# GpSimd takes norms, diagonal blocks and part of a convolution in a fused two-layer kernel on Trainium2

## The reference

```
mixed   = silu(conv4(x @ W_qkv.T))          # causal, depthwise, 4 taps, 2048 channels
q, k, v = split(mixed)                      # 8 key heads (each for 2 value heads), 16 value heads, 64 wide
z, beta = x @ W_z.T, sigmoid(x @ W_b.T)
g       = -exp(A_log) * softplus(x @ W_a.T + dt_bias)
per token:  S = S * exp(g);  delta = (v - S'k) * beta;  S = S + k delta';  o = S'(q / 8)
h       = o * silu(z);  h = h * rsqrt(mean(h*h) + 1e-6) * norm_weight
out     = h @ W_out.T
```

## Time and profile before

| | us |
|---|---|
| median of three executions | 1510.51 (1510.26 to 2404.46) |
| profiled execution | 1512.68 |
| its span in the trace | 1510.9 |
| PE busy | 1284.2 (85%) |
| DVE busy | 910.1 (60%) |
| ACT busy | 726.2 (48%) |
| POOL busy | 194.1 (13%) |

### The profile page before, as it was taken

How to read it: one execution, slowest core, us unless ns; L and a number is a source line. 1 busy time by engine, 2 the same in 40 slices (tenths; PEclk the granted TensorE clock), 3 DMA queues, 4 the chain that set the end, 5 groups by cost and what they waited for, 6 DMA issues and landing times.

```text
span 1510.9 us, 26872 instructions
## 1 busy us (share of the span) xinstructions
PE 1284.2 (85%) x11048; PEld 928.8 (61%) x11048; DVE 910.1 (60%) x2365; ACT 726.2 (48%) x1353; POOL 194.1 (13%) x186
## 2 busy tenths in 40 slices
PE   2668889798898979889996959998899989989899
PEld 2355767576575756757765536665567656666566
DVE  4897888979788897969255333552445523463321
ACT  1648375665746556582541324434352354523442
POOL 5111221212112121212010010000100000000000
PEclk9768779788877978887898788998999999999999
DMA  4000000000000000010120000000000000000000
GB/s 125 4 2 5 0 2 11 2 12 1 12 1 2 11 2 8 2 32 8 54 105 8 2 1 0 1 8 1 8 0 8 1 2 8 0 1 1 1 8 7
DMA packets 15066, 17.69 MB, mean 12 GB/s; under 512 B 2567, under 2 KB 13216, under 8 KB 14560
## 3 DMA queue, kind: packets, MB, share of 16 engines
q1 hardware_dynamic: 12768, 14.09, 2.8%
q0 software_dynamic: 576, 1.76, 0.4%
q10 hardware_dynamic: 1600, 0.12, 0.1%
HBM read 13.87 MB, written 2.10 MB: 11 GB/s over the span
## 4 chain that ended last, share of the span: by engine, by line
PE 60%; DVE 25%; ACT 9%; issue 3%; POOL 1%; DMA 1%; SPq 0%; DVEq 0%; ACTq 0%
PE ps L1539 8%; PE ps L1529 8%; PE ps L1329 7%; PE ps L1094 4%; DVE arena L1880 4%; DVE arena L1883 3%; DVE arena L1797 3%; PE ps L1237 3%; PE ps L1112 3%; DVE arena L2154 2%; ACT arena L975 2%; PE ps L1631 2%; PE ps L1170 2%; PE ps L1595 2%; PE ps L1259 1%
## 5 line engine op out<-in xcount | busy, mean ns | idle before, releaser
L1797 DVE SCALAR_TENSOR_TENSOR arena<-ps,conv_w,arena 128x255 f32<-128x255 f32 (+2 forms) x384 | 163.8, 475 | 19.1 <-ACT arena L636 14.5
L937 ACT ACTIVATE arena<-ps 128x512 f32<-128x512 f32 x144 | 85.3, 597 | 180.7 <-PE ps L1529 180.7
L1539 PEld LDWEIGHTS ps<-arena 128*128 128x128 f32 x1152 | 132.6, 192 | 24.8 <-issue 9.9
L1539 PE MATMUL ps<-arena 128*128 128x128 f32 x1152 | 136.9, 277 | 7.1 <-ACT arena L937 4.1
L1529 PE MATMUL ps<-arena 128*128 128x512 f32 x288 | 134.3, 612 | 0.0
L2125 DVE SCALAR_TENSOR_TENSOR arena<-ps,gates,arena 128x128 f32<-128x128 f32 x128 | 36.0, 344 | 113.7 <-PE ps L1539 113.4
L523 POOL TENSOR_TENSOR rstd<-var_eps,half_power 128x2 f32<-128x2 f32 (+1 forms) x28 | 23.3, 833 | 621.1 <-DVE var_eps L1768 621.1
L2191 DVE TENSOR_REDUCE arena<-ps 128x8 f32<-128x2048 f32 (+1 forms) x24 | 54.8, 2292 | 62.8 <-PE ps L1595 62.8
L1529 PEld LDWEIGHTS ps<-arena 128*128 128x128 f32 x288 | 51.4, 194 | 61.0 <-issue 44.8
L1883 DVE TENSOR_TENSOR arena<-arena 128x30 f32<-128x30 f32 (+14 forms) x240 | 83.4, 348 | 8.2
L502 POOL TENSOR_TENSOR arena<-con,log_decay 128x512 f32<-128x512 f32 x64 | 67.0, 1059 | 162.6 <-PE ps L1094 62.1
(11 more groups left out here) (246 smaller groups left out, 2817.2 us busy)
## 6 DMA issues: line engine op xcount, KB each, us to landing
arena<-in_routed_up SPq DMA_DIRECT2D x1, 2048.0 KB, 10.5
arena<-in_routed_down SPq DMA_DIRECT2D x1, 2048.0 KB, 14.9
x_ln<-in_x SPq DMA_DIRECT2D x8, 128.0 KB, 2.3
arena<-in_w_mix SPq DMA_DIRECT2D x1, 1024.0 KB, 10.9
x_in<-in_x SPq DMA_DIRECT2D x8, 128.0 KB, 2.3
out_x<-x_res SPq DMA_DIRECT2D x8, 128.0 KB, 1.9
arena<-out_x SPq DMA_DIRECT2D x4, 256.0 KB, 2.7
out_x<-arena SPq DMA_DIRECT2D x4, 256.0 KB, 2.2
```

What stands on the lines that cost most here:

```text
L937: act.activation(hid1[half][:, i, :], ps[:, banks[i], :], ACT.Gelu).then_inc(s["mgelu"], 1)
L1539: mm = pe.matmul(ps[:, bank, c * P:(c + 1) * P], hid1[half][:, i, c * P:(c + 1) * P], m_down[:, e, i, :], start=(i == 0), stop=(i == HT1 - 1))
L1797: ins = dve.scalar_tensor_tensor(conv_tile(f, m)[:, sh:SEQ], ps[:, PAIR_BANK[p], j * SEQ:(j + 1) * SEQ - sh], conv_w[:, m, TAPS - 1 - sh:T ...
```

## The change

Four things are moved, and the waits around them follow.

1. `log_decays(f, 0..2)` on VectorE stand between `products(n, 3)` and `products(n, 6)` and no longer behind all products; `exponents` goes ahead of `products(n, 3)`. On TensorE `turn_norm` and `beta_decay` come first in a round, `decay_sums(n, 3)` goes from the end of a round to the start of the next, and so do the second chunk's `turn_heads`. ScalarE's list follows, and its `diagonal_blocks(n, 1)` is split: three quarters once seven products are there, the last quarter after the eighth.
2. `normalise` goes from VectorE to GpSimd, behind each `root_of_squares`.
3. `unit_blocks` goes from ScalarE to GpSimd, two blocks ahead of the first masks of sequence f and two behind the second.
4. For the channel pairs 0 to 4 (`TAPPED = 5`) ScalarE writes a second copy, the tile times its second tap (`second_tap`), into one of two buffers in `xs64`, and GpSimd adds it, one position shifted, to the seed (`add_tap`); VectorE adds two taps in place of three to these pairs.

```diff
-HT_BANKS = ((6, 6), (7, 2))
+HT_BANKS = (6, 7)
...
+TAPPED = 5
...
+        tap = [xs64[:, 8 * r:8 * (r + 1), :].rearrange("p (j b) d -> p j (b d)", j=2) for r in range(2)]
...
         @block.gpsimd
+            def add_tap(f, p):
+
+                pool.wait_ge(s["seeded"], f * MIX + 2 * p + 2)
+                pool.wait_ge(s["tapped"], 2 * (TAPPED * f + p + 1))
+                both = mix_qk[f % 2][:, 2 * p:2 * p + 2, 1:SEQ] if p < QK_TILES else mix_v[:, 0:2, 1:SEQ]
+                pool.tensor_tensor(both, both, tap[p % 2][:, :, 1:SEQ], ALU.add).then_inc(s["tap_added"], 1)
...
+            def normalise(i, c):
+
+                pool.wait_ge(s["o_rstd_ready"], CH * i + c + 1)
+                pool.tensor_tensor(hz_slot(i, c), hz_slot(i, c), over_last(o_rstd[:, :], DH), ALU.mult)\
+                    .then_inc(s["hn_ready"], 1)
+
+            def unit_blocks(n, q):
+
+                pool.wait_ge(s["uc_ready"], n + 1)
+                after(pool, "e_psum", 4 * n)
+                r = slice(BLOCK * q, BLOCK * (q + 1))
+                pool.tensor_scalar(um[r, :, r], uc[r, :, :], -1.0, None, ALU.mult).then_inc(s["um_blocks"], 1)
...
                 if has_i:
                     root_of_squares(i, 0)
+                    normalise(i, 0)
+                if has_f:
+                    for p in range(TAPPED):
+                        add_tap(f, p)
+                if has_i:
                     root_of_squares(i, 1)
+                    normalise(i, 1)
+
+                if has_n:
+                    pool.wait_ge(s["gm_ready"], CH * NB * (n + 1))
+                    after(pool, "hn_ready", CH * (i + 1))
+                    if has_f:
+                        pool.wait_ge(s["tap_added"], TAPPED * (f + 1))
+                    unit_blocks(n, 2)
+                    pool.wait_ge(s["um_blocks"], QUADS * n + 1)
+                    unit_blocks(n, 3)
+                    pool.wait_ge(s["um_blocks"], QUADS * n + 2)
...
-                if has_f:
-                    for k in range(NB + 1):
+                if has_f:
+                    masked_decays(f, 0)
+                    masked_decays(f, 1)
+                    pool.wait_ge(s["gm_ready"], CH * NB * f + 2)
+                if has_n:
+                    unit_blocks(n, 0)
+                    pool.wait_ge(s["um_blocks"], QUADS * n + 3)
+                    unit_blocks(n, 1)
+                    pool.wait_ge(s["um_blocks"], QUADS * n + 4)
+                if has_f:
+                    for k in range(2, NB + 1):
                         masked_decays(f, k)
...
         @block.scalar
+            def second_tap(f, p):
+
+                after(act, "tap_added", TAPPED * f + p - 1)
+                after(act, "b64_psum", 4 * (f - 1))
+                for j in range(2):
+                    m = 2 * p + j
+                    act.activation(tap[p % 2][:, j, 1:SEQ], ps[:, PAIR_BANK[p], j * SEQ:(j + 1) * SEQ - 1], ACT.Copy,
+                                   scale=conv_w[:, m, TAPS - 2:TAPS - 1]).then_inc(s["tapped"], 1)
...
-                act.wait_ge(s["at_ready"], CH * NB * n + NB * (c + 1))
...
-                for q in range(QUADS):
-                    r = slice(BLOCK * q, BLOCK * (q + 1))
-                    act.activation(atc[r, hs, :], at[r, hs, r], ACT.Copy).then_inc(s["atc_ready"], 1)
+
+                for lo, hi in ((0, NB),) if c == 0 else ((0, NB - 1), (NB - 1, NB)):
+                    act.wait_ge(s["at_ready"], CH * NB * n + NB * c + hi)
+                    for q in range(QUADS):
+                        r = slice(BLOCK * q, BLOCK * (q + 1))
+                        act.activation(atc[r, hs, :].rearrange("p (g y) n -> p g y n", g=2)[:, :, 2 * lo:2 * hi, :],
+                                       at[r, hs, r].rearrange("p (g y) n -> p g y n", g=2)[:, :, 2 * lo:2 * hi, :], ACT.Copy)\
+                            .then_inc(s["atc_ready"], 1)
...
+                if c == 0 and g == 0 and n + 1 < SEQS:
+                    act.wait_ge(s["tap_added"], TAPPED * (n + 2))
...
                 if has_f:
                     seed(f, 0)
+                    second_tap(f, 0)
                     seed(f, 1)
+                    second_tap(f, 1)
...
-                    unit_blocks(n, 2)
-                    unit_blocks(n, 3)
...
-                    unit_blocks(n, 0)
-                    unit_blocks(n, 1)
...
         @block.tensor
+                if has_f:
+                    turn_norm(f)
+                if has_n:
+                    decay_sums(n, 3)
+                if has_f:
+                    beta_decay(f)
+                if has_i and i > 0:
+                    turn_heads(i - 1, 1, 0)
                 if has_n:
                     decay_sums(n, 4)
                     key_products(n, 3)
-                if has_f:
-                    turn_norm(f)
+                if has_i and i > 0:
+                    turn_heads(i - 1, 1, 1)
...
-                if has_f:
-                    beta_decay(n, f, has_n)
...
         @block.vector
             def convolve(me, f, p):
 
                 dve.wait_ge(s["seeded"], f * MIX + 2 * p + 2)
-                for sh in range(1, TAPS):
-                    if sh > 1:
+                first = 2 if p < TAPPED else 1
+                if p < TAPPED:
+                    dve.wait_ge(s["tap_added"], TAPPED * f + p + 1)
+                for sh in range(first, TAPS):
+                    if sh > first:
...
+                if has_f:
+                    exponents(me, f)
+                if has_n:
                     products(me, n, 3)
+                if has_f:
+                    log_decays(me, f, 0)
+                if has_n:
                     products(me, n, 4)
+                if has_f:
+                    log_decays(me, f, 1)
+                if has_n:
                     products(me, n, 5)
                 if has_f:
-                    exponents(me, f)
+                    log_decays(me, f, 2)
...
-                if has_i:
-                    normalise(i, 0)
...
-                if has_i:
-                    normalise(i, 1)
```

More of the change, by code:

```diff
@@ L681, in second_block @@
                     .then_inc(s["t2_ready"], 1)
-            def unit_blocks(n, q):
-                act.wait_ge(s["uc_ready"], n + 1)
-                after(act, "e_psum", 4 * n)
-                r = slice(BLOCK * q, BLOCK * (q + 1))
-                act.activation(um[r, :, r], uc[r, :, :], ACT.Copy, scale=-1.0).then_inc(s["um_blocks"], 1)
             def merged32(n, c):
@@ L1026, in turn_norm @@
                 after(pe, "conv_done", NP * f - 1)
-                after(pe, "hzT_ready", 4 * (f - 2))
                 for c in range(CH):
@@ L1030, in turn_norm, with beta_decay @@
                 mm.then_inc(s["d_hT_psum"], 1)
-            def beta_decay(n, f, has_n):
+            def beta_decay(f):
                 pe.wait_ge(s["d_hT_ready"], f + 1)
-                if has_n:
-                    pe.wait_ge(s["gam_ready"], n + 1)
                 for c in range(CH):
@@ L1212, in solve @@
                     pe.wait_ge(s["u64_ready"], 4 * (i + 1))
+                    pe.wait_ge(s["um_blocks"], QUADS * (i + 1))
                     pe.wait_ge(s["vtok_ready"], 4 * (i + 1))
@@ L1337, in _ @@
                     key_products(n, 3)
-                if has_f:
-                    turn_norm(f)
+                if has_i and i > 0:
+                    turn_heads(i - 1, 1, 1)
+                if it == SEQS - 1:
+                    up_tile(0, 4)
                 if has_n:
@@ L1453, in _ @@
                     key_products(f, 2)
-                    decay_sums(f, 3)
                 if it == SEQS - 1:
@@ L1457, in _ @@
                     up_tile(0, 11)
[L1458 to L1464 removed]
+            turn_heads(SEQS - 1, 1, 0)
+            up_tile(0, 12)
+            turn_heads(SEQS - 1, 1, 1)
             project_out(SEQS - 1, SEQS, 1, False)
@@ L1915, in sum_squares @@
                 dve.wait_ge(s["hz_sq"], CH * i + c + 1)
+                after(dve, "o_rstd_ready", CH * i + c)
                 me.did(dve.tensor_reduce(ssq[:, :], squared(i), X_AXIS, ALU.add))
@@ L2027, in _ @@
                     products(me, n, 2)
-                    products(me, n, 3)
-                    products(me, n, 4)
-                    products(me, n, 5)
                 if has_f:
@@ L2033, in _ @@
                 if has_n:
+                    products(me, n, 3)
+                if has_f:
+                    log_decays(me, f, 0)
+                if has_n:
+                    products(me, n, 4)
+                if has_f:
+                    log_decays(me, f, 1)
+                if has_n:
+                    products(me, n, 5)
+                if has_f:
+                    log_decays(me, f, 2)
+                if has_n:
                     products(me, n, 6)
                     products(me, n, 7)
-                if has_f:
-                    log_decays(me, f, 0)
+                if it == SEQS - 1:
+                    product_of_tile(0, 4)
                 if has_i and i > 0:
```

(5 more changed lines are left out.)

78 lines of the change are left out of this document (32 added, 46 removed).

## The result

The changed kernel takes 1542.29 us (median of four, 1538.33 to 1544.75) beside 1510.38 for the kernel before on the same chip: a ratio of 1.0217, interval 1.0188 to 1.0245. It is 32 us slower. The profiled execution took 1544.75 us with a span of 1542.9, so the spans differ by 32.0.

The account below looks back on a forecast made before the run. TensorE and VectorE were taken to share the bound, so the round's chain of waits was priced: +0.8 + 0.6 + 5.05 - 0.35 = +6.1 us a full round, +39.8 in all, forecast 1550 us, range 1507 to 1573.

Parts of the forecast that it names:

- C: Taps: five GpSimd additions a round hold VectorE's steps_of_inverse 1.01 us each, +5.05 us; VectorE's saved work becomes idle time.
- Rival 2: Additions cost the weighted rows' price, 3.0 us a round, and normalise 0: +3.45 a round, 1532 us; chance 0.13.
- rival 1: GpSimd waits instead of VectorE, so B gives -1.2 and C 0: -0.75 us a round, 1504 us; chance 0.12.
- The wait ahead of `solve32`: Sign on TensorE behind the gates: its wait would go up from 4.8 us by a few.
- Rival 3: TensorE's clock: if part (c) runs at 2.4 GHz, +2.7 us a round, 1529 us; chance 0.06.
- part (c): Round's last stretch, from 364.7: TensorE and ScalarE hand each other inverse blocks until the last convolution seeds and their silu.
- part (b): Round's middle stretch, 341.5 to 364.6, VectorE alone: steps_of_inverse, first normalise, gated, the transposes.
- A: Log decays between the products and diagonal_blocks split: +0.8 us a round, between -1.0 and +1.7.
- B: Normalise on GpSimd: first one's 1.22 us leaves VectorE, 1.8 held; net +0.6 us a round, between 0 and +0.8.
- the prediction's other estimate: Skill's GpSimd ratio of 1.96 for an elementwise pair: normalise would take about 2.4 us, total 3 to 4 us more.
- D: unit_blocks off ScalarE: last seeds start 0.4 us sooner, GpSimd's cost hidden; -0.35 us a round, between -1.0 and 0.
- The sum: +6.1 us per full round, six times +36.6; with the other rounds +39.8 on the profiled 1512.7 us.

Follow-up runs that it names:

- the fill: The changed kernel with each GpSimd tap addition replaced by a memset of about the same duration that reads nothing, leaving out five pairs' second tap: 1509.5 us.
- the kernel with the late `hn_ready`: The changed kernel without taps, normalise on VectorE, only the first log_decays piece between products, `hn_ready` wait kept ahead of unit_blocks: 1537.1 us.

## Why the prediction was right, and where it was off

The forecast was 1550 us and slower; the measured time is 1542, inside the range. The mechanism of part C was right and carries the result.

**C** was put at 5 x 1.01 us a round. One addition holds VectorE for 1.01 us, the idle time ahead of the sixth pair is 5.99 us (5.7 predicted), and the fill shows that nothing else in the taps counts. Rival 2's price of 0.6 us for each is out, and rival 1 (GpSimd is the one that waits) is too: its additions take 1.27 us, and VectorE's steps take the stretch. The wait ahead of `solve32` did not grow by a few us: it is 5.25 in place of 4.83. The prediction took 1.01 from a like row and had no reason why it isn't 1.27. The ends of the steps give one: the wait lasts to the end of the addition, and only the start of the step and 0.15 us of its own work save something. (The whole 1.27 us for each addition would come to 9 us more in all, not 8: seven rounds have additions.)

**The clock** is not the cause. Rival 3 is out, since part (c) ran at 0.54, 0.51 before. In part (b) what counts is `outputs`, which the first `gated` operations wait for: 3.68 us at a granted clock of 1.00 (the level of 2.4 GHz), 6.93 at 0.50 (1.2 GHz). Before, four of the six rounds had the longer one, after, two (it = 3 and 4; it = 0 has 4.43). So the lower level came less often after the change, but it costs more where it comes. In rounds at 1.00 VectorE waits for nothing between the transposes, before and after, and the stretch grows from 40.0 to 45.9 us. In rounds at 0.50 it waited 0.9 to 2.2 us before and waits 4.4 us after (2.65 of it at 437.27), and the stretch grows from 41.6 to 50.3. Why a round gets the one or the other isn't settled; in the 13 us ahead of the `v_tokens` of the two rounds shown TensorE did the same work, group by group.

**A** was put at +0.8 a round. Its marks came as predicted: the last product 2.1 us late (2.1 predicted), the transpose 0.8 us early (1.0). `v_tokens` come 5.4 us behind the last product, 5.6 before: the split gives 0.2 back, not 0.5. And `gated` does what was said of it: where it waits for `outputs`, the earlier transpose is lost, and where it doesn't, it is kept. (The round that the prediction read, it = 2, changed sides: `outputs` took 6.93 us in it before and 3.68 after, and its wait of 0.76 us is gone.) But the step that explained the late product was wrong. It charged the log decays with nearly all of it and the new order of TensorE with 0.3 us. Alone the order makes 1.4 of the 2.1 us and costs 20 us in all; with the log decays put back, 1.8 of the 2.1 remain, and the kernel is 8 us slower. That A still came out near its forecast is luck: a cost of the order that was put too low stands against a gain of the log decays that was taken for a cost. The parts don't add, so their prices alone say nothing of A. The singles (order +20.0, normalise +3.2, unit blocks -8.4) and -1.0 for everything but the taps leave -16 for the log decays and the split together, while the two runs that bear on them gave -8 for the log decays, beside the taps, and +8 for the split, beside the unit blocks.

**B** was put at +0.6 with 1.8 us held. 1.58 are held, so +0.36 at the step; by the stretch of the transposes it is +0.6. GpSimd takes 2.02 us for the operation that is met, not the 2.4 of the prediction's other estimate.

**D** was put at -0.35. It is worth 1.2 us a round by the total of its run (8.4 over seven) and by ScalarE's rows. The step that failed is the size of "those behind seed 5 let the last seeds start 0.4 us sooner": from the seed of the sixth pair to that of the seventh it is 4.1 us before (380.26 to 384.37) and 3.1 in the kernel with unit blocks alone (372.42 to 375.54), 1.0 sooner, because that pair of copies stood ahead of a merge that the seventh pair waits for. The two ahead of `solved64` gave 0.2. `unit_blocks` at 2.76 us on GpSimd are hidden, as said, though near the upper bound given (2.85). That cover has an end, as the kernel with the late `hn_ready` shows.

**The sum** was +39.8 and came out at 32. In the rounds it = 0 to 4 it was +6.1 each and +4.84 was measured. Of the 1.26 us too many, 0.4 are D's by the marks (-0.8 for -0.35) and the rest is A's and B's, which gave +0.6 together where +1.4 was forecast. That makes 6.3 us in five rounds. The start and the round it = -2 gave -3.1 for -1.5, and the end of the rounds -0.3 for +1.0. Against these stand 1.3 us from it = 5 and 0.2 from it = -1. Together these are the 7.8 us.

## What to carry to other kernels

Work moved to GpSimd isn't off VectorE's time when both read SBUF at once: a step that starts beside a GpSimd operation ends only after it, so count the operation's whole time, less a few tenths of a microsecond, as time of VectorE, and move it to where VectorE reads from PSUM or is idle. Offload only what VectorE is the last to finish; saved work ahead of a wait becomes idle time. When several moves come in one change, test each alone and in company: here the order costs 20 us alone, and together with all the other moves but the taps it costs nothing that shows. And compare rounds that had the same granted clock; a mean over rounds mixes two kinds.

## What the runs showed of the hardware

- A VectorE operation with two inputs in SBUF that starts beside a GpSimd addition or product is held to that operation's end: 35 steps beside the additions (128x510, 1.27 us) and seven beside `normalise` (128x1024, 2.02 us) end 0.25 to 0.27 us after it. Held are 1.01 and 1.58 us. In the earlier trace rows a 30-element step takes 0.49 us for 0.19; the `weighted` operation beside it lasts 0.64 us, started 0.21 before the step and ended 0.07 before the step's end. So the hold is no fixed share of the GpSimd operation. The Trainium skill, "SBUF — State Buffer", section "SBUF: two separate sides", speaks of an exclusive lock for the whole instruction; the trace agrees for these operations, and the hold that one counts is shorter by the late start and by the last part of the step itself. It does not agree for the root: that is an operation with two SBUF inputs too (128x16), and in its 2.98 us no step is held.
- A GpSimd fill of 1.27 us holds no step of the inverse, as the root doesn't: the largest steps beside both keep their 0.40 to 0.41 us. But beside the fill a scaling of 128x32 with one input in SBUF takes 1.09 us for 0.18; the same operation beside an addition takes 1.12 (at 29.88 in the changed kernel).
- An addition doesn't hold VectorE while it reads one of two operands from PSUM: 0.43 us for an operation of the convolution beside four additions.
- The 32 matmuls of `outputs` take 3.68 us at a granted clock of 1.00 and 6.93 at 0.50, and rounds of the same loop get the one or the other.
- A scaled copy of 32x1024 takes 2.76 us on GpSimd and 1.05 on ScalarE.
